# Graph attention and product-key attention: ScalarE's row transfers in two places of a unit

## The reference

```python
def gnn(h, adj, W, a):
    Wh = h @ W
    e = Wh @ a[:D] + swapaxes(Wh @ a[D:], 1, 2)
    e = where(e > 0, e, 0.2 * e)
    e = where(adj > 0, e, -inf)
    return elu(softmax(e) @ Wh)

def ffn(x):
    q = (x @ Wq).reshape(b, n, HEADS, DIM) * DIM ** -0.5
    kv_scores, indices = pk(x)          # top 16 of two 128-key sets, top 16 of their sums, softmax
    ind = indices + offsets
    k = einsum('bnhk,bnhkd->bnhd', kv_scores, keys_table[ind])
    v = einsum('bnhk,bnhkd->bnhd', kv_scores, values_table[ind])
    attn = softmax(causal(einsum('bihd,bjhd->bhij', q, k)))
    return einsum('bhij,bjhd->bhid', attn, v).reshape(b, n, HEADS * DIM) @ Wo

x = x + gnn(layernorm(x))
x = x + ffn(layernorm(x))
```

## Time and profile before

| | |
|---|---|
| median of 3 runs | 9993.5 us (9992.27 to 9996.31) |
| profiled execution, its own time | 9991.23 us |
| its span | 9989.4 us |
| mean granted TensorE clock | 0.748 |
| POOL busy | 7483.0 us (75%), 7894 instructions |
| DVE busy | 6973.1 us (70%) |
| PE busy, PEld busy | 5695.5 us (57%), 4494.4 us (45%) |
| ACT busy | 3117.2 us (31%), 9834 instructions |
| transfers of table rows by SP, by ACT | 22,304 and 18,016 |

### The profile page before, as it was taken

How to read it: one execution, slowest core, us unless ns; L and a number is a source line. 1 busy time by engine, 2 the same in 40 slices (tenths; PEclk the granted TensorE clock), 3 DMA queues, 4 the chain that set the end, 5 groups by cost and what they waited for, 6 DMA issues and landing times.

```text
span 9989.4 us, 208546 instructions
## 1 busy us (share of the span) xinstructions
PE 5695.5 (57%) x23108; PEld 4494.4 (45%) x23108; DVE 6973.1 (70%) x42908; ACT 3117.2 (31%) x9834; POOL 7483.0 (75%) x7894
## 2 busy tenths in 40 slices
PE   5666565555655555555565555655556555555555
PEld 4444444444444444444444444444444444444444
DVE  8777677767777677676776776767767777666664
ACT  4333333333333333333333333333333332322222
POOL 5677777777777777777777777777777777777776
PEclk7777777777777777777777777777777777777777
DMA  3344343333433334333343333433334333333333
GB/s 111 101 110 110 110 114 110 110 110 110 114 110 110 110 110 114 110 110 110 110 114 110 110 110 112 112 110 110 110 112 112 110 110 110 110 112 110 110 110 99
DMA packets 525949, 1101.84 MB, mean 110 GB/s; under 512 B 213120, under 2 KB 271104, under 8 KB 524320
## 3 DMA queue, kind: packets, MB, share of 16 engines
q0 software_dynamic: 378096, 1032.96, 36.4%
q1 hardware_dynamic: 83248, 37.82, 1.6%
q10 hardware_dynamic: 63104, 18.63, 0.9%
HBM read 1084.36 MB, written 4.19 MB: 109 GB/s over the span
## 4 chain that ended last, share of the span: by engine, by line
POOL 72%; issue 24%; ACTq 1%; DVE 1%; PE 1%; POOLq 0%; DMA 0%; ACT 0%; SPq 0%; DVEq 0%
POOL ring L366 72%; ACTq L508 1%; DVE hot L1036 0%; DMA wo<-in_Wo 0%; POOLq L382 0%; POOLq L380 0%; ACTq L503 0%; PE ps_o L749 0%; DMA far_row<-far_at 0%; PE ps_s L718 0%; PE ps_p L632 0%; DMA ring<-in_table,idx 0%; DVE ps_v L958 0%; ACT diag L457 0%; PE ps_p L636 0%
## 5 line engine op out<-in xcount | busy, mean ns | idle before, releaser
L366 POOL DMA_INDIRECT ring<-in_table,idx x7877 | 7481.5, 950 | 2479.1 <-issue 2401.0
L693 PE MATMUL ps_w<-ring,diag 128*128 128x256 f32 x8192 | 2109.9, 417 | 11.1 <-DMA ring<-in_table,idx 8.9
L693 PEld LDWEIGHTS ps_w<-ring,diag 128*128 128x128 f32 x8192 | 1710.9, 214 | 280.4 <-issue 13.0
L1036 DVE SCALAR_TENSOR_TENSOR hot<-rank,posf,cand 128x54 f32<-128x54 f32 x8192 | 1659.9, 270 | 0.3
L705 PE MATMUL ps_t<-ident,kv 128*128 128x128 f32 x448 | 192.2, 429 | 2370.2 <-DVE kv L969 2370.2
L955 DVE TENSOR_SCALAR ps_v<-ring,wgt 128x256 f32<-128x256 f32 x512 | 248.5, 485 | 1801.7 <-DMA ring<-in_table,idx 1799.4
L958 DVE SCALAR_TENSOR_TENSOR ps_v<-ring,wgt,ps_v 128x256 f32<-128x256 f32 x3072 | 1475.8, 480 | 19.6
L457 ACT ACTIVATE diag<-ident,wgt 128x128 f32<-128x128 f32 x4096 | 1251.9, 391 | 0.0
L705 PEld LDWEIGHTS ps_t<-ident,kv 128*128 128x128 f32 x448 | 75.7, 169 | 2481.4 <-DVE kv L969 2481.4
L749 PEld LDWEIGHTS ps_o<-probT,kv 128*128 128x128 f32 x4480 | 972.6, 312 | 309.8 <-ACT probT L474 245.1
L749 PE MATMUL ps_o<-probT,kv 128*128 128x128 f32 x4480 | 986.7, 401 | 193.4 <-ACT probT L474 193.1
(11 more groups left out here) (125 smaller groups left out, 8211.5 us busy)
## 6 DMA issues: line engine op xcount, KB each, us to landing
far<-in_table SPq DMA_DIRECT2D x22304, 1.0 KB
far<-in_table ACTq DMA_DIRECT2D x18016, 1.0 KB
ring<-in_table,idx POOLq DMA_INDIRECT x7877
xin<-in_x SPq DMA_DIRECT2D x8, 512.0 KB
mask<-in_adj SPq DMA_DIRECT2D x1, 4096.0 KB, 13.8
out_x<-acc SPq DMA_DIRECT2D x64, 64.0 KB
far_row<-far_at ACTq DMA_DIRECT2D x188, 0.5 KB
far_row<-far_at SPq DMA_DIRECT2D x127, 0.5 KB
```

The lines of the kernel that those rows point to most:

```text
L366: pool.indirect_dma_start(out=ring[:, t % RING, k, :], out_offset=None, in_=table, in_offset=bass.IndirectOffsetOnAxis(ap=idx[:, t, k:k + ...
L693: ins = nc.tensor.matmul(pw_ps, diag[:, k, :], ring[:, t % RING, k, :], start=(k == 0), stop=(k == PE_ROWS - 1))
L1036: c = step(nc.vector.scalar_tensor_tensor(out=hot[:, k, :], in0=rank[:], scalar=posf[:, k:k + 1], in1=cand[:, 1, :], op0=ALU.is_equal, op1 ...
```

## The change

The first two places at which ACT issues transfers of table rows are taken away: 8 ahead of the probability copies and 8 behind them. The third, 8 behind the diagonals, stays. The last, at the end of the unit, issues what is left, which was 12 and is now 28.

```diff
-TURNING = 8
-TURNED = 8
 SUMMING = 8
@@
                         choose_begin(n1 // HEADS if graph else BATCH - 1, n1 * UNITS + t1, t1)
-                    some(fetch, TURNING)
                     if t or not first:
                         attend_turned(*behind)
-                    some(fetch, TURNED)
                     if ahead:
                         choose_softmax((n + 1) * UNITS + t)
                     attend_begin(n, t)
```

## The result

The changed kernel takes 10,023.4 us (median of 7 runs, 10,017.9 to 10,042.7) and the kernel before 9,995.4 us (7 runs, 9,992.3 to 9,998.5). The ratio is 1.0031 [1.0022, 1.0041]. It is slower by 28 us. The forecast was 211 us slower, so the direction holds and the size does not. The profiled execution took 10,019.97 us, 28.7 us above the one before.

The account below looks back on a forecast made before the run. POOL's gathers bound the kernel at 154.3 us a head; ACT's terms sum to 156.5 us, falling 2.2 us behind each head. With 16 us a batch for the projection that adds 211 us: 10,202 us, range 9,985 to 10,400.

Parts of the forecast that it names:

- The gearing: ACT's loop against POOL's pace over the batches: each microsecond in ACT's 156.5 us head is worth 55 us of time.
- the start: POOL's single wait of 21.9 us for a sum of the first head: some 6 us of it go away.
- the projection: Between two batches on ACT: it adds 16 us to the loop, which heads no longer win back.
- a point at 152.3 us: ACT's time for a head at which it is decided between no change and ACT setting the pace.
- 8 plain units, transfers and queue: ACT's transfers, address load and small queue steps: 14.7 us in a unit, 117.6 us in a head.
- exponential to kT: ACT's queue stands still while PE transposes and turns keys: mean 2.75 us a unit (2.5 to 3.05), 22.0 us a head.
- new waits behind kT: ACT's query copy waits for PE's values and scores: 3.9 us a head at full clock, 11 at half, 7.0 taken.
- address DMA, its wait in unit 1: ACT's waits from issuing the address DMA to the first transfer: between 1 and 7 us stay a head, 3.3 taken.
- square root, head end, graph copies, rest: The rest of ACT's head, as before: 2.8 us, 3.3 us and 0.5 us, together 6.6 us.
- ACT stays inside its slack: Rival: PE at full clock, ACT's head 149.7 us, below POOL's 154.3, so no change, 9,986 us; chance 0.22.
- Half clock everywhere: Rival: PE at half clock throughout, ACT's head 166.6 us, about 10,760 us; chance 0.05.
- slower gathers: Rival: 28 transfers in a row meet POOL's descriptors, 0.01 us on each gather, about 10,070 us; chance 0.03.

Follow-up runs that it names:

- 16 transfers behind the diagonals: The changed kernel with 16 transfers behind the diagonals in place of 8, so 20 at the end and not 28: 9987.4 us, ratio 0.9994 to the kernel before.
- 28 added matmuls: The changed kernel with 28 identity matmuls in each unit on PE ahead of its wait for the exponential, their result overwritten: 9982.1 us, ratio 0.9989.
- both halves of this one: The kernel before without only the 8 transfers behind the probability copies: 10,218.1 us; without only the 8 ahead of them: 10,091.6 us.
- graph sum late: The changed kernel with PE's graph sum of unit 3 moved to the end of the unit: 10,017.4 us, ratio 1.0026.
- increments in unit 6: The changed kernel with 20 increments of an unused semaphore and one clear on ACT's queue in unit 6 of each head: 10,105.3 us, ratio 1.0109.

## Why the prediction was right in direction and wrong in size

**The gearing was right.** The loss comes from ACT's loop against POOL's, and at the batch ends. With the measured 153.4 us and 13.1 us in the prediction's own sum, a head adds nothing, a batch loses 5.5 us, six lose 33, the start gives 6, and the result is +27. Measured is +28. Wrong were the length of the loop, 3.1 us a head, and the projection, 2.9 us a batch, and with them the case: ACT neither lies inside its slack nor falls behind in each head. It lies between 152.7 us, (1234.8 - 13.1) / 8, and 154.3 us a head, where it wins some back and not enough. The prediction had a point at 152.3 us from which loss begins, and saw no case of its own between there and 154.3 us.

**The terms of a head**, predicted and measured, from means over the units of six batches:

| term | predicted | measured |
|---|---|---|
| 8 plain units, transfers and queue | 117.6 | 117.0 |
| exponential to kT | 22.0 | 22.9 |
| new waits behind kT | 7.0 | 2.1 |
| address DMA, its wait in unit 1 | 3.3 | 1.4 |
| square root, head end, graph copies, rest | 6.6 | 10.0 |
| head | 156.5 | 153.4 |
| projection | 16 | 13.1 |

**The step that failed is "new waits behind kT", 7.0 us.** It rested on 5.7 us for the widest unit, with 3.17 us for the values "at the full clock". Those 3.17 us were a row at 0.50, as shown above. In the changed order the same matmuls took 1.86 us in the unit shown, where PE runs from the transposes through without the gap of 0.93 us that the probability copies made before, and 2.3 in the median. The sum should have read 0.15 until PE starts, 1.86 to 2.3, 1.88 and 0.4, some 4.3 to 4.7 us against 4.4 us of ACT's own count. Measured over that count are 1.0 us in the unit with the graph sum, some 0.5 in the units 6 and 7, and little elsewhere. The upper bound of 11 us, with the scores at the half clock in every unit, did not occur either: the scores of 8 tiles took 1.88 us in the median, 2.20 before. The change moves the half clock, it does not add it everywhere: transposes of 7 tiles went from 0.99 to 1.76 us (medians), values and scores became faster.

**That the direction came out right is in part luck.** With this one term put right, the prediction's own sum gives 156.5 - 4.9 = 151.6 us a head and 8 x 151.6 + 16 = 1228.8 us a batch, under POOL's 1234.8, and so no loss. The loss that was measured also needs the 3.4 us by which the rest of a head was taken too short.

**Exponential to kT** came out as 22.9 us, within its bounds of 2.5 to 3.05 a unit. The argument was that PE would be idle and its transposes more often at the half clock. The Trainium skill (TensorE: Matmul & The Clock Gate, What's actually happening) has PE throttled by default and released by activity. The trace agrees: 7.42 us of idle time, then 0.50, and 0.94 a few microseconds later. The prediction placed this rule at the transposes only, though it holds just as well for what comes behind them.

**The address DMA and the rest** were off by 1.9 and 3.4 us with opposite signs. The DMA lies beside kT, its diagonals and the unit's waits, and costs 1.4 us:

```profile
5135.06 0.53 ACTq L488 DMA_DIRECT2D far_row<-far_at  x1
...
5139.10 2.79 ACTq L506 DMA_DIRECT2D far<-in_table  x8
```

That is 4.0 us from issue to transfer, 8.5 in the late stretch of before. The head end came from the first batch, where it has no table load. The six batches behind it have one at each head end, ahead of the copy of the query weights:

```profile
5267.01 1.28 ACT L447 ACT_TABLE_LOAD   x1 [13.29 <-issue]
5268.30 0.30 ACT L447 COPY wq_cur<-wq 128x128 f32 x1
5269.39 1.11 ACT L464 ACTIVATE prob<-ps_s,nmax 128x1024 f32<-128x1024 f32 x1 [0.79 <-issue]
```

With it the head end takes 5.4 us (median) in place of 3.3. The square root takes the 2.8 us that I had, and 1.8 us are graph copies and what is left, where I had 0.5. I had taken the head end of one batch for all.

**The rivals.** "ACT stays inside its slack" came close: its 149.7 us were 3.7 below what was measured, but its time of 9,986 us is what the run with 16 transfers behind the diagonals took (9987.4). "Half clock everywhere" did not occur, nor did slower gathers (950 ns in both; their distance grew by 0.0004 us, 3.0 us in all). The Trainium skill (Trainium Kernel Development and Optimization, Key Constraints) says that issuing from several engines saves only the issue time. No run here moves transfers between engines. What these runs show is that the place of the issue time in one queue matters: the same transfers gave 9987 and 11,815 us.

**What was foretold of the profile.** The copies wait for PE, kT follows the exponential by 1.6 to 4.2 us, and the next exponential follows kT by 14.6 to 20.4 us (medians of the eight units). DVE's waits for rows shrank, further than said, and the catch-up of the first 1000 us is gone. POOL's stops of some 200 us did not come: 22.8 us of waits for sums and 37.0 us at the batch ends. Neither sign of being wrong came either: POOL's waits with those stops are over 78 us, and no head of the first batch behind the first is under 152 us.

What is not settled: why the 28 added matmuls brought 1.2 us a head when most transposes stayed at the half clock, and what sets the distance of the gathers in an execution.

## What to carry to other kernels

A queue of transfers between two compute instructions is cover for another engine's work: ask of each place what it hides, and what is late if it moves, and test the whole change, since both halves of this one were slower than the whole. Before a row's duration is used as a price, read the granted clock of that very stretch, and ask whether the change fills or opens the gap ahead of it. When a loop runs near another's pace, work out the case between the two decision points too, for there the loss is a fraction of what the next microsecond costs.

## What the runs showed of the hardware that was not expected

- The same 14 values matmuls of 128x128 in f32 took 3.17 us at 0.50 and 1.86 us mostly at 1.00. Ahead of the 3.17 us there was no long wait: PE was busy for 1.02 of 3.60 us, still at a mean of 0.93, with 0.93 us of idle time at the end.
- 28 matmuls of 3.22 us in the idle stretch did not keep the clock: after a further 4.20 us of idle time the transposes were at 0.50.
- The mean distance of POOL's gathers was 1.2549 us in the kernel before and 1.258 us in the profiled executions of four other kernels (16 behind the diagonals, 28 added matmuls, graph sum late, increments in unit 6), while a fifth, on the same chip as three of them, had 1.255. For the kernel with 16 transfers behind the diagonals that execution took 10,011.8 us, its other nine 9984.1 to 9988.5. 7877 x 0.003 is 24 us, which is the difference. What sets it stays open.
- Address loads that the kernel text has and whose values nothing uses are not in the trace (1001 loads with and without them), so they can't serve as a delay. 20 increments of a semaphore took 1.3 to 1.5 us of ACT's queue (medians of three kernels), and their unit became 1.3 us longer in the changed kernel.
